# Attention with q and k in three bfloat16 parts: each part stored once, and repeated by the loads

## The reference

```python
x = _ln(src) * (1.0 + scale) + shift
q = (x @ Wq + bq).reshape(B, S, N_HEAD, HEAD_DIM).transpose(0, 2, 1, 3)
k = (x @ Wk + bk).reshape(B, S, N_HEAD, HEAD_DIM).transpose(0, 2, 1, 3)
v = (x @ Wv + bv).reshape(B, S, N_HEAD, HEAD_DIM).transpose(0, 2, 1, 3)
scores = jnp.einsum('bhqd,bhkd->bhqk', q / math.sqrt(HEAD_DIM), k)
scores = scores + attention_bias
scores = jnp.where(src_mask, -jnp.inf, scores.astype(jnp.float32))
probs = jax.nn.softmax(scores, axis=-1).astype(v.dtype)
ctx = jnp.einsum('bhqk,bhkd->bhqd', probs, v)
```

## Time and profile before

| | us |
|---|---|
| median of 3 runs | 1013.82 |
| lowest, highest | 1010.88, 1017.82 |
| the profiled execution, its device time | 1015.7 |
| its span, first to last instruction | 1013.9 |

### The profile page before, as it was taken

The page is one execution under the profiler, slowest core; times in us unless marked ns, Lnnn a source line. Parts: engine busy times, 40 slices in busy tenths (PEclk is TensorE's granted clock), DMA queues, the critical chain, the costliest instruction groups (busy, mean ns, idle before and its releaser), DMA issues.

```text
span 1013.9 us, 19565 instructions
## 1 busy us (share of the span) xinstructions
PE 975.4 (96%) x6670; PEld 735.7 (73%) x6736; DVE 840.8 (83%) x1983; ACT 749.9 (74%) x1234; POOL 691.0 (68%) x365
## 2 busy tenths in 40 slices
PE   7999999999899999999999999999998899999998
PEld 5889988999665655656656565656565699999897
DVE  5799999997968999999999999999999655555562
ACT  6654675546689999999999999999998544444444
POOL 3567766765166988989989899997997744444210
PEclk9999999999999999999999999999999999999999
DMA  8757779869999999999999999999998522221001
GB/s 262 245 162 250 259 264 336 286 230 327 376 301 405 391 393 398 366 390 370 385 364 362 373 362 390 365 359 364 345 358 257 136 85 68 73 75 42 22 22 42
DMA packets 141396, 275.26 MB, mean 271 GB/s; under 512 B 19938, under 2 KB 76002, under 8 KB 141170
## 3 DMA queue, kind: packets, MB, share of 16 engines
q1 hardware_dynamic: 140866, 273.93, 76.3%
q10 hardware_dynamic: 432, 0.07, 0.0%
HBM read 222.03 MB, written 51.92 MB: 270 GB/s over the span
## 4 chain that ended last, share of the span: by engine, by line
PE 58%; ACT 24%; DVE 5%; DMA 5%; issue 3%; POOL 3%; SPq 1%; POOLq 0%; DVEq 0%; ACTq 0%
PE psH L613 16%; PE psO L613 16%; ACT t_bt L948 14%; PE psT L729 10%; ACT t_pt L838 7%; PE psV L742 4%; PE psS L718 4%; PE psQ L613 3%; DMA t_ks<-sc_qk 3%; PE psA L613 2%; SPq L276 1%; POOL t_bt L1475 1%; ACT t_mb L970 1%; ACT t_cv L838 1%; DVE t_y L1094 1%
## 5 line engine op out<-in xcount | busy, mean ns | idle before, releaser
L1475 POOL TENSOR_TENSOR t_bt<-t_bt,t_mb 128x1024 f32<-128x1024 f32 x198 | 418.8, 2154 | 53.3 <-DMA t_bt<-in_fside_Bx16xSxS 53.1
L1277 DVE CUSTOM_DVE_ANT_0 t_bt<-psS,t_bt 128x512 f32<-128x512 f32 x512 | 338.2, 687 | 29.6 <-PE psS L718 27.9
L948 ACT ACTIVATE t_bt<-t_bt,t_nm 128x512 f32<-128x512 f32 x512 | 346.1, 722 | 4.5 <-DVE t_nm L1277 4.5
L729 PE MATMUL psT<-t_idf,t_bt 128*128 128x128 f32 x2048 | 309.5, 274 | 9.9 <-ACT t_bt L948 8.1
L729 PEld LDWEIGHTS psT<-t_idf,t_bt 128*128 128x128 f32 x2048 | 250.3, 141 | 70.2 <-ACT t_bt L948 20.9
L718 PE MATMUL psS<-t_ks,t_qs 128*128 128x512 bf16 x466 | 177.2, 380 | 6.4 <-DMA t_ks<-sc_qk 3.5
L838 ACT ACTIVATE t_pt<-psT 128x512 f32<-128x512 f32 x268 | 159.9, 597 | 24.2 <-PE psT L729 23.5
L1287 DVE COPY t_pt<-psT 128x512 f32<-128x512 f32 x244 | 167.6, 687 | 5.5 <-PE psT L729 5.5
L742 PE MATMUL psV<-t_pt,t_vs 128*17 128x512 f32 x1024 | 135.0, 601 | 0.0
L718 PEld LDWEIGHTS psS<-t_ks,t_qs 128*128 128x128 bf16 x512 | 49.9, 97 | 90.2 <-DVE t_nm L1277 84.8
L875 ACT ACTIVATE psH<-psH,t_bi 128x512 f32<-128x512 f32 x64 | 42.3, 662 | 69.1 <-PE psH L613 66.0
(11 more groups left out here) (176 smaller groups left out, 1937.6 us busy)
## 6 DMA issues: line engine op xcount, KB each, us to landing
t_bt<-in_fside_Bx16xSxS SPq DMA_DIRECT2D x256, 512.0 KB, 7.5
sc_qk<-t_parts SPq DMA_DIRECT2D x64, 384.0 KB, 6.6
t_qs<-sc_qk SPq DMA_DIRECT2D x64, 256.0 KB, 6.2
t_ks<-sc_qk SPq DMA_DIRECT2D x64, 256.0 KB, 7.1
t_wo_f<-in_L_cond_Wo SPq DMA_DIRECT2D x8, 1024.0 KB, 6.1
sc_qk<-t_parts SPq DMA_DIRECT2D x32, 256.0 KB, 8.2
t_wi_f<-in_L_cond_Wi SPq DMA_DIRECT2D x7, 1024.0 KB, 8.9
sc_v<-t_v SPq DMA_DIRECT2D x8, 544.0 KB, 8.0
```

What stands on the lines that cost most here:

```text
L729: ins = e.transpose(psT[turned_bank(n)][:, kk, :], bt[u % NB][:, t, kk * 128:(kk + 1) * 128], idf[:, :])
L948: e.activation(p, p, ACT.Exp, bias=nm[:, n % NR:n % NR + 1], scale=-1.0).then_inc(a_exp, 1)
L1277: e.tensor_tensor_reduce(bt[u % NB][:, t, :], s, bt[u % NB][:, t, :], -1.0, 3.0e38, ALU.add, ALU.min, nm[:, n % NR:n % NR + 1]).then_inc(v ...
L1475: e.tensor_tensor(bt[u % NB][:, hs, :], bt[u % NB][:, hs, :], mb[b % 2][:, hs, :], ALU.add).then_inc(g_M, 1)
```

## The change

sc_qk now holds each part once: [batch, q or k, half, part, 128, 512]. Part 0 is stored by half as soon as it is made, parts 1 and 2 with both halves in one DMA, so 8 stores per batch instead of 12, without a repeat. The repeat moves to the loads. A piece is now four heads (4 KB per row) and takes five DMAs: q's part 0 to partitions 0 to 47 (repeated three times), part 1 to 48 to 95 (three times), part 2 to 96 to 127 (twice), k's three parts to partitions 0 to 95 (the three of them repeated twice), and k's parts 0 and 1 to 96 to 127. There are two pieces per half batch, at its tiles 4 and 16; the first set is issued at tiles 20 and 21. The last batch's parts are stored at tiles 28 to 112 in steps of 12, k's first, and the waits for these stores move from tile 236 to tiles 104 (k) and 184 (q).

```diff
-PT = 16 * 6
+PT = 16 * 4
...
-QK_STEP, ROWS_AT = 6, (184, 248, 312, 376, 440)
+QK_STEP, ROWS_AT = 12, (184, 248, 312, 376, 440)
...
-        sc_qk = dram("sc_qk", [B, 2, NK, NP3, 128, S], BF16)
+        sc_qk = dram("sc_qk", [B, 2, NK, 3, 128, S], BF16)
...
-        late_stores = range(28, 28 + 12 * 12, 12)
+        late_stores = range(28, 28 + 8 * 12, 12)
...
                 if a == 0:
                     P.wait_ge(a_p0, 4 * b + 2 * n + mt + 1)
-                elif a == 1:
-                    P.wait_ge(a_p1, 2 * b + n + 1)
+                    load(d_p[b % 2][n], sc_qk[b, n, mt, 0], parts[b % 2][n][:, 0, mt, :])
                 else:
-                    P.wait_ge(g_p2, 2 * b + n + 1)
-                g = slice(a, NP3, 3) if n else slice(3 * a, min(3 * a + 3, NP3))
-                k = len(range(NP3)[g])
-                load(d_p[b % 2][n], sc_qk[b, n, mt, g].rearrange("i p s -> p i s"), parts[b % 2][n][:, a:a + 1, mt, :].broadcast_to([128, k, S]))
+                    if a == 1:
+                        P.wait_ge(a_p1, 2 * b + n + 1)
+                    else:
+                        P.wait_ge(g_p2, 2 * b + n + 1)
+                    load(d_p[b % 2][n], sc_qk[b, n, :, a].rearrange("m p s -> p m s"), parts[b % 2][n][:, a, :, :])
...
-                hs = slice(2 * i, 2 * i + 2)
+                hs = slice(4 * i, 4 * i + 4)
...
-                for dst, w in ((qs, 0), (ks, 1)):
-                    load(d_q[n % 2], dst[n % 2][:, hs, :], sc_qk[b, w, half].rearrange("i (d h) s -> (i d) h s", d=HD)[:, hs, :])
+                q, k = (sc_qk[b, w, half].rearrange("a (d h) s -> a d h s", d=HD)[:, :, hs, :] for w in range(2))
+                for a in range(3):
+                    z = min(3 * a + 3, NP3)
+                    load(d_q[n % 2], qs[n % 2][3 * a * HD:z * HD, hs, :], q[a:a + 1].broadcast_to([z - 3 * a, HD, 4, S]))
+                load(d_q[n % 2], ks[n % 2][0:6 * HD, hs, :], k.rearrange("a d h s -> (a d) h s").unsqueeze(0).broadcast_to([2, 3 * HD, 4, S]))
+                load(d_q[n % 2], ks[n % 2][6 * HD:KR, hs, :], k[0:2].rearrange("a d h s -> (a d) h s"))
...
-                    store_part(B - 1, i // 2 % 2, i // 4, i % 2)
+                    store_part(B - 1, 1 - i // 4, max(i % 4 - 1, 0), i % 4)
...
+                if n == 104:
+                    P.wait_ge(d_p[1][1], PT * B // 2)
+                if n == ROWS_AT[0]:
+                    P.wait_ge(d_p[1][0], PT * B // 2)
...
-                if n == 236:
-                    for w in range(2):
-                        P.wait_ge(d_p[1][w], PT * B // 2)
...
-                if n < N and 0 <= m < 4 * step and m % step == 0 and n // 32 + 1 < 2 * B:
+                if n < N and 0 <= m < 2 * step and m % step == 0 and n // 32 + 1 < 2 * B:
...
-                P.wait_ge(d_q[g % 2], 128 * (g // 2 + 1))
+                P.wait_ge(d_q[g % 2], 160 * (g // 2 + 1))
```

More of the change, by code:

```diff
@@ L335, in store_part @@
                     P.wait_ge(a_p0, 4 * b + 2 * n + mt + 1)
-                elif a == 1:
-                    P.wait_ge(a_p1, 2 * b + n + 1)
-                else:
-                    P.wait_ge(g_p2, 2 * b + n + 1)
-                g = slice(a, NP3, 3) if n else slice(3 * a, min(3 * a + 3, NP3))
-                k = len(range(NP3)[g])
-                load(d_p[b % 2][n], sc_qk[b, n, mt, g].rearrange("i p s -> p i s"), parts[b % 2][n][:, a:a + 1, mt, :].broadcast_to([128, k, S]))
+                    load(d_p[b % 2][n], sc_qk[b, n, mt, 0], parts[b % 2][n][:, 0, mt, :])
+                else:
+                    if a == 1:
[3 more added lines that the diff above has]
+                    load(d_p[b % 2][n], sc_qk[b, n, :, a].rearrange("m p s -> p m s"), parts[b % 2][n][:, a, :, :])
             def store_parts(b, a):
-                for i in range(4):
-                    store_part(b, i // 2, a, i % 2)
+                for n in range(2):
+                    for mt in range(1 if a else NK):
+                        store_part(b, n, a, mt)
             def store_v(b):
@@ L428, in first_attention_loads @@
                 load_mask(0)
-                for i in range(4):
+                for i in range(2):
                     load_qk(0, i)
```

## The result

The changed kernel takes 1529.06 us in the median (1527.47 to 1533.11), the kernel before beside it 1013.64: 1.507 times as long, 95% interval 1.503 to 1.511. The forecast said slower, by 370 us; it became slower by 515. The sign held, and so did the cause that it named, loads on few DMA engines; the time lies outside the range of 1320 to 1500.

The account below looks back on a forecast made before the run. TensorE was taken to bound the attention, with a full DMA behind it. Loads on few engines make a half batch 32.2 + 23.4 = 55.7 us, so half 15 begins 368 us later: 1015.7 + 368 = 1384 us, range 1320 to 1490.

Parts of the forecast that it names:

- Few engines: q/k loads: uneven sides put them on 3, 3, 2, 2 and 16 engines; packets under 512 B fall to 18,210.
- sixteen engines: Rival, q/k loads: destination rows alone decide, so all 16 engines share every load; about 1010 us, chance 0.11.
- Other engines each time: Rival, q/k loads: each load on few engines takes the next ones, evening the load; 1020 to 1060 us, chance 0.02.
- The start of the attention: First scores wait 32.2 us for the first q/k set and begin at about 272 us instead of 256.6.
- Removed stores worth 0, at most 10 us: Stores before and early in the attention: 21 MB less, worth 0 to 10 us, taken as 0.
- The sum's term for a half batch: Attention, busiest engines: q and k 32.2 us plus the rest 23.4, so 55.7 us a half against TensorE's 31.2.
- half 15: Last half batch of the attention: begins at 1120 us instead of 751.8, or at 1197 with 22.9 GB/s.
- The rate: A never idle DMA engine in the attention moves 24.9 GB/s; the low end, 22.9 GB/s, gives 1461 us.
- The engines never run dry: Attention: bias queues behind q and k on the same engines, which stay busy and set the attention's pace.
- nothing overlaps: Rival, attention: SP's issue stalls, bias follows q/k; 63.4 us a half, 1487 us; chance 0.05 together with the low clock.
- The clock: Rival, attention: gaps keep TensorE at 1.2 GHz, matmuls 61 us a half, about 1484 us; chance 0.05 with nothing overlaps.
- Tiles of 1.7 us in the mean: Sign for the forecast, attention; tiles at 1.0 us behind long waits at each half would speak against it.

Follow-up runs that it names:

- rows16: Changed kernel with q's and k's repeats written out as loads of their own, 11 even loads per piece instead of 5; 1095.5 us, ratio 1.079.
- block16: Changed kernel with 16 loads per piece, one per term of q and k, each 16 rows into 16 neighbouring partitions; 1100.2 us, ratio 1.084.
- copies16: Kernel before with its eight stored copies, loaded by 16 loads of 16 rows per piece of four heads; 1112.8 us, ratio 1.097.
- heads4: Kernel before with pieces of four heads at tiles 4 and 16, in loads of 128 rows, nothing else of the change; 1011.6 us, ratio 0.997.
- half_after: Changed kernel with half of the bias left out after the first five heads, each load bringing one of its two tiles; 1337.6 us.
- early: Changed kernel with both pieces of a half batch issued at tiles 4 and 5 instead of 4 and 16; 1462.8 us, ratio 1.440.
- tiny: heads4 with 14 added transfers of 1 KB, memory to memory, behind each piece; 1143.2 us, ratio 1.127.

## Why the prediction was right and wrong

**Few engines: right.** To the packet (18,210) for the changed kernel, and to one packet for rows16 (23,011 for 23,010). The rival *sixteen engines* falls with it. *Other engines each time* would send the same packets; it falls with the share of 0.57, where it wanted 1.0, and with the time, where it wanted 1040 us.

**The start of the attention: right.** First scores at 269.8 us, forecast 272.

**Removed stores worth 0, at most 10 us: about right.** block16 has them removed and copies16 doesn't, with the same loads otherwise: 1100.2 and 1112.8, so 13 us where the DMA is short, about the forecast's most. At TensorE's pace it was not tried. The new piece size and places alone (heads4) gained 0.3%, just clear of the noise.

**The sum's term for a half batch: wrong, and this is the whole miss.** The step that failed is "Then q and k cost 32.2 us a half on these engines and the rest 23.4: 55.7 us". It measured 65.2. Over the 14 steady halves that is 133 us, and the longer first half has the rest; half 15 was to begin at 1120 and began at 1265.9, 146 us late, and 1529 − 1384 is 145. Behind that point all went as said. Two things in that step were mis-sized:

The rate. I took 24.9 GB/s for an engine, from the best 30 us of the trace, and argued that idle engines leave the memory to the busy ones. The windows give 19.4 GB/s for a busy engine, half_after 19.3, and the whole half 1.386 MB / 65.2 us = 21.3 on the busiest. In the packet records a 4 KB packet takes 160 ns in the median in both kernels, but 209 ns in the mean of the steady halves, against 171 before. With at most 2.5 packets under way at a time it is 166, and with 14 and more 215. So the engines are as quick as I took them while few work, and slower than before when all are at work. The even loads of few rows (block16, 213 ns) show the same lengthening without the uneven sides. Why, no run shows. The low end that I kept, 22.9 GB/s and 1461 us, was still too fast.

"The engines never run dry". That holds nearly (fewer than two packets are under way for 1.7% of the steady halves), but it doesn't follow that the order costs nothing. The place of the second piece is worth 66 us in the whole run (early), which a sum of bytes can't have. SP's issue of the small k load, the one behind the large load on two engines, takes 7.0 us in the median and up to 9.5, against 0.46, as if it had to wait for room on these two, and SP issues no bias for the other fourteen meanwhile. The forecast knew this as the rival *nothing overlaps*, 63.4 us a half and 1487 in all, and gave it 0.05 together with the clock. It came nearest in size (65.2), but isn't the mechanism in the changed kernel: there half of the bias bytes still took 13.6 us off a half. It comes near early, where they took 4.1.

What share of the 9.5 us is slower packets and what is SP held up, the runs don't separate. Both act on the same engines, and half_after changes both.

**The clock.** The forecast wrote that a granted clock under 0.9 through the attention would mean that TensorE's clock is the price. It is 0.77 from 600 to 1000 us, and the sentence was wrong as a test: the clock is low in and right after the stalls (0.50 to 0.70 in the windows of 840 to 856 us), and PE is idle for 189 of these 400 us for want of data. The first scores behind a stall take 0.61 us instead of 0.38. PE's busy time grew by 68 us in all, 4 us for each half, and a half grew by 34. So my estimate is that the clock took no more than these 4. It was not tried apart. The rival's own time for the low clock, 1484, doesn't follow from its terms: 61 us a half from 272 us on give 1451.

**Tiles of 1.7 us in the mean** were 2.04 (65.2 / 32), in the form that the forecast had put under "wrong": tiles at full pace behind long waits.

## What to carry to other kernels

A repeat in the outermost place of one side of a DMA sets how many engines carry it. Keep the slowest dimension on both sides divisible by 16, and count the closing packets, 16 for each transfer, to see it. Where a transfer fills two engines, ask what the issuing queue does at the next transfer that needs them, and what stands behind it there; don't price it at the rate of the best stretch (here even that of the loaded one, 22.9 GB/s, was too high). And the cure has a price too: where the DMA is full, loads of one to three rows for each engine had longer packets (208 to 213 ns against 170), and many issues can fill the issuing queue itself (tiny). So few large even transfers (heads4, 1011.6 us) beat many small even ones (1095 to 1143).

## What the runs showed of the hardware

- An issue on SP is not a fixed cost: 0.42 to 0.46 us for even loads, 0.73 for the uneven q loads, 0.61 for the k load that puts 196,608 B on each of two engines, and 7.0 in the median, up to 9.5, for the small load of 32 rows right behind it.
- 28 transfers of 1 KB for each half batch, with no use and almost no bytes, cost 132 us of 1012: SP then spends 36.5 of 39.5 us on issues, and the DMA share falls to 0.87.
- Loads of one to three rows for each engine had 4 KB packets of 208 to 213 ns in the mean, with all engines busy, where loads of eight rows for each engine with the same bytes had 170.
- The same bytes left out were worth 192 us in one order of the loads (1529.1 to 1337.6) and 71 in the other (1462.8 to 1391.9), so that the order that was slower with all of them became the faster one.
- A share above 1 doesn't mean full rate: block16 has 1.07 at 232 GB/s in one stretch and 1.03 at 372 just before it.
